# A cross-attention kernel: its four chunks of queries in the order 1, 3, 2, 0 instead of 1, 2, 3, 0

## What is computed

```
q = LN(x) @ Wq.T ; k = ctx @ Wk.T ; v = ctx @ Wv.T            # 16 heads of 16
scores = q k.T / 4 ; masked keys and keys after the query's own row -> -inf
attn = softmax(scores) ; context = attn @ v
x = x + (sigmoid(LN(x) @ Wg.T + bg) * context) @ Wo.T
scale = the two largest of softmax(LN(x) @ gate_w), others 0  # 8 experts
x = x + sum_e (silu(s_e xn @ w1_e) * (s_e xn @ w3_e)) @ w2_e  # xn = LN(x), s_e = its scale
```

## Time and profile before

| | us |
|---|---|
| three runs | 688.59, 688.75, 693.32 (median 688.75) |
| the profiled execution | 690.36 |
| its span, from first to last instruction | 688.6 |
| mean granted TensorE clock, share of full speed | 0.963 |

### The profile page before, as it was taken

How to read it: one execution, slowest core, us unless ns; L and a number is a source line. 1 busy time by engine, 2 the same in 40 slices (tenths; PEclk the granted TensorE clock), 3 DMA queues, 4 the chain that set the end, 5 groups by cost and what they waited for, 6 DMA issues and landing times.

```text
span 688.6 us, 13557 instructions
## 1 busy us (share of the span) xinstructions
PE 653.8 (95%) x5320; PEld 377.0 (55%) x5320; DVE 469.9 (68%) x969; ACT 385.0 (56%) x778; POOL 242.9 (35%) x293
## 2 busy tenths in 40 slices
PE   7897999999989999999999999999999996899996
PEld 3354455455545445444554445545456675688884
DVE  5684778999866999989987975454423354645452
ACT  2212676766634777777566877677875640232331
POOL 5004123422140305020211614527164535566563
PEclk9898999999996999999999999999999998899997
DMA  6984766010700000000770101003010011012000
GB/s 169 242 118 84 130 129 79 2 21 33 114 11 1 3 3 2 2 33 32 96 181 1 35 1 31 2 3 108 2 44 21 16 33 62 31 62 90 34 31 30
DMA packets 29305, 36.58 MB, mean 53 GB/s; under 512 B 5833, under 2 KB 16457, under 8 KB 29242
## 3 DMA queue, kind: packets, MB, share of 16 engines
q1 hardware_dynamic: 26248, 34.53, 23.7%
q10 hardware_dynamic: 946, 0.92, 0.4%
q0 software_dynamic: 2048, 0.27, 0.3%
HBM read 25.58 MB, written 8.06 MB: 49 GB/s over the span
## 4 chain that ended last, share of the span: by engine, by line
PE 74%; POOL 9%; DVE 7%; issue 6%; ACT 4%; POOLq 0%; ACTq 0%; DVEq 0%
PE bank L1566 18%; PE bank L1544 14%; PE bank L1511 11%; PE bank L1395 11%; PE bank L1630 3%; POOL h_lo L1022 3%; POOL v_sb L1018 3%; PE bank L1632 2%; PE bank L1631 2%; DVE pmax L1284 2%; POOL xn_sb L994 2%; ACT probs L1150 2%; PE bank L1515 2%; DVE v_sb L1374 2%; PE bank L1470 2%
## 5 line engine op out<-in xcount | busy, mean ns | idle before, releaser
L1284 DVE TENSOR_REDUCE pmax<-bank 128x1 f32<-128x512 f32 (+6 forms) x640 | 327.5, 578 | 69.3 <-PE bank L1515 46.8
L1150 ACT ACTIVATE probs<-bank 128x512 f32<-128x512 f32 (+4 forms) x592 | 287.4, 545 | 138.0 <-PE bank L1544 86.8
L1566 PE MATMUL bank<-probs,vaug 128*32 128x256 f32 (+4 forms) x2048 | 156.1, 396 | 0.5 <-ACT probs L1150 0.5
L1544 PE MATMUL bank<-qaug,kaug 64*128 64x512 f32 (+4 forms) x592 | 149.0, 452 | 7.0 <-DVE pmax L1284 3.2
L1511 PE MATMUL bank<-kaug,qaug 62*128 62x512 f32 (+6 forms) x640 | 139.6, 414 | 3.1 <-DVE pmax L1284 1.6
L1544 PEld LDWEIGHTS bank<-qaug,kaug 64*128 64x128 f32 (+1 forms) x592 | 64.4, 185 | 82.3 <-ACT probs L1150 29.8
L1511 PEld LDWEIGHTS bank<-kaug,qaug 62*128 62x128 f32 x640 | 70.7, 189 | 56.5 <-DVE pmax L1284 21.3
L1032 POOL TENSOR_SCALAR nmax<-rmax 128x16 f32<-128x16 f32 x16 | 5.2, 323 | 235.3 <-DVE rmax L1292 235.3
L1566 PEld LDWEIGHTS bank<-probs,vaug 128*32 128x32 f32 (+1 forms) x2048 | 46.5, 109 | 52.1 <-issue 31.1
L1202 ACT ACTIVATE h_hi<-v_sb 128x512 fp32r<-128x512 f32 x32 | 20.2, 632 | 80.5 <-DVE v_sb L1374 79.4
L1022 POOL TENSOR_TENSOR h_lo<-v_sb,h_hi 128x512 fp32r<-128x512 f32 x32 | 41.2, 1288 | 61.3 <-ACT h_hi L1202 61.3
(11 more groups left out here) (137 smaller groups left out, 790.2 us busy)
## 6 DMA issues: line engine op xcount, KB each, us to landing
qaug<-s_dram SPq DMA_DIRECT2D x32, 256.0 KB, 3.3
qaug<-q_parts SPq DMA_DIRECT2D x18, 256.0 KB, 9.2
q_parts<-stage SPq DMA_DIRECT2D x7, 512.0 KB, 2.9
k_parts<-stage SPq DMA_DIRECT2D x4, 512.0 KB, 5.3
w_sb<-in_w SPq DMA_DIRECT2D x4, 512.0 KB, 11.0
out<-x_sb SPq DMA_DIRECT2D x8, 256.0 KB, 2.2
ctx_sb<-in_ctx_t SPq DMA_DIRECT2D x3, 512.0 KB, 5.7
x_sb<-in_x SPq DMA_DIRECT2D x3, 512.0 KB, 6.9
```

What stands on the lines that cost most here:

```text
L1150: act.activation(probs[0:rows, u % NSLOT, h, off:CH], bank_of(e)[0:rows, off:CH], ACT.Exp, scale=DK ** -0.5).then_inc(act_read, 1)
L1284: dve.tensor_reduce(pmax[:, n % 2, qt, h, slot:slot + 1], bank[:, 0:w], AX_X, ALU.max).then_inc(dve_read, 1)
L1544: last.append(pe.matmul(pair[side][0][0:r, off:CH], keys_at(b, ROWS, hp, P * j, r), qaug[b:b + ROWS, p % 2, hp, off:CH], start=True, stop= ...
L1566: last = pe.matmul(psum[O_BANK][32 * h:32 * h + 32, q0:q1], vaug[0:r, col:col + 32], probs[0:r, u % NSLOT, h, q0:q1], start=(j == 0), stop ...
```

## The change

The chunks go in the order 1, 3, 2, 0. Position 1 is now chunk 3 and position 2 chunk 2. Chunk 3 needs all keys, so position 1's list holds the projections of key chunks 2 and 3 and value tiles 8 to 12, and position 2's list holds none of these. The two key chunks are read back by one `kload` step: SyncE waits for all four stores, then issues 12 DMAs. The second `kload` step, that of position 2, is gone. All sizes and instruction counts stay the same; `make_plan` is run anew, so the order in which each engine meets its work may differ everywhere.

```diff
-ORDER = (1, 2, 3, 0)
+ORDER = (1, 3, 2, 0)
...
-KEYS_OF = ((0, 1), (2,), (3,), ())
+KEYS_OF = ((0, 1), (2, 3), (), ())
 FIRST_M = (1, 0, 0, 0)
-FIRST_TILE = (0, 8, 12, KT, KT)
+FIRST_TILE = (0, 8, KT, KT, KT)
...
     steps = [*norm]
     for k in KEYS_OF[p]:
-        steps += [("kq", "k", 0, k), ("kq", "k", 1, k), ("kload", p)]
+        steps += [("kq", "k", 0, k), ("kq", "k", 1, k)]
+    if KEYS_OF[p]:
+        steps.append(("kload", p))
```

## The result

The changed kernel takes 702.86 us (median of 4 runs, 700.59 to 708.52); the kernel before, on the same chip, 691.04 (4 runs, 688.59 to 694.45). The ratio is 1.0176, 95% interval 1.0124 to 1.0228: slower by 12 us. The forecast was 690, with a range up to 702.

A forecast was written before the change was run, and what follows sets the result against it. VectorE's maxima were taken to pace the long stretch (126.0 to 420.8 us) and TensorE's experts the end. To the profiled 690.4 us the terms added only 1.7, giving 692.1, or 690 against the median; range 676 to 702.

The forecast's parts named there:

- The loads move into the head: Before group 4: extra key stores and loads delay position 1's queries by at most 8.6 us, covered by 10.1; cost 0.
- Rival 4: In the head: the loads aren't covered and group 4 begins some 4 us late, 694 us; chance 0.05.
- VectorE's term 0: Long stretch, 126.0 to 420.8 us: the same 448 reduces with the same shapes after the swap, so 0 change.
- Exponentials behind larger folds: At group 5: ScalarE waits 0 to 3.4 us for the fold of 64 reduces; 1.7 taken.
- Less left at the end: After the long stretch: 8 fewer exponentials in groups 10 and 11, but 358 still run before 420.8; 0, bound -7.0 us.
- The experts' gate: Group 8's exponentials end 9.9 us later, so the first experts begin near 402 and 434; cost 0, bound 9.9 us.
- Rival 2: From the experts on: their gate decides, experts 0 to 3 come up to 9.9 us late, 700 us; chance 0.20.
- Rival 1: Near 203 us: the new list fills TensorE's wait for position 0's layer norm, gaining 11.9 us, 678.5; chance 0.24.
- Rival 3: One more stall of the kind at 203 us, costing 7.2 us, 697 us; chance 0.07.

The follow-up runs named there:

- fold_first: The changed kernel with SyncE holding position 1's twelve key loads until group 1's fold has landed, all lists kept; 709.70 us, ratio 1.0261.
- split_keys: The changed kernel with key chunks 2 and 3 loaded by separate steps, each after its own stores; 698.77 us, ratio 1.0079.
- k3_late: The changed kernel with key chunk 3's projections, stores and loads behind position 1's queries, the two chunks loaded apart; 695.37 us, ratio 1.0039.
- joint_old_order: The changed kernel with the old order 1, 2, 3, 0 and value tile 12 left in place, both key chunks still loaded together; 706.93 us, ratio 1.0203.
- after_st4: The changed kernel with the scheduler allowed to run four `st` (score tile) items ahead instead of three; 724.94 us, ratio 1.0475.
- big_loads_alone: The changed kernel with key chunk 3's six small loads issued behind the query loads, lists and stores kept; 707.96 us, ratio 1.0231.

## Why the prediction was wrong, point by point

**The step that failed** is "The loads move into the head": the cost put at 0 under a cover of 10.1 us, with a worst case of 8.6. Its first half was right: the key loads went out 8.2 us later (84.22 against 76.03), by two more turns of the stores. But the query loads went out 16.2 us later, not 8.6 at most, and the last of them landed at 131.4. That is 5.4 us after the 126.0 at which group 4 began before, so the cover was gone, and by the step's own rule 5.4 of the 7.2 us would have come from this alone.

Two terms were missing. The step counted SyncE's queue and left the query projections where they were on TensorE. The new list put the first of them 11.1 us later. And the fold of group 1 wasn't in the account, whose four DMAs go out from GpSimd's queue at 88.1 to 89.7, the time to which the large loads had been moved. TensorE waited 4.39 us for it and ran at the lower clock after it. By the same list in fold_first this cost 6.4 us up to group 4's first scores, beside the late queries and not on top of them. Rival 4 named the right place, at 4 us and a chance of 0.05.

What the head costs in all can only be read from kernels whose lists differ: 1.4% (9.5 us) in the new order and 2.0% (14 us) in the old. Group 4's start accounts for 6.3 (133.2 - 126.9) and 7.6 us (136.1 - 128.5) of these. The rest lies behind it, in lists that were made anew, and no run takes it apart. Nor is group 4's start in split_keys (132.1) explained by a wait: its queries are in by 126.2 and the fold holds nobody, but TensorE is busy for 118.9 us up to there, in k3_late for 112.8.

**VectorE's term 0** was right: 449 reduces in 231.96 us, the stretch 0.6 us shorter.

**Exponentials behind larger folds**, 0 to 3.4 us, taken as 1.7: no such wait came. ScalarE's timeline of the kernel after at the change from group 4 to group 5:

```profile
242.63 3.27 ACT L1152 ACTIVATE probs<-bank 65x512 f32<-65x512 f32 x6 [0.41 <-PE bank L1551]
246.47 1.08 ACT L1152 ACTIVATE probs<-bank 128x512 f32<-128x512 f32 x2 [0.56 <-PE bank L1546]
```

The row of six holds the four of group 4's last key tile (65 keys) and two of the next group, without a gap between them, and the next wait is 0.56 us. I had group 4 done at 210.9; the list let it run until 245, and what the next group then waits for is TensorE's scores, no DMA.

**Less left at the end**: the assumption that as many exponentials run beside the maxima (358) was wrong, 331 did. It cost less than the 10.4 us of the second stretch suggest: k3_late left as many (196) and was within 0.4% of the kernel before.

**The experts' gate**: forecast 402 and 434, measured 423.94 and 456.95, of which 7.2 us come from the head. Rival 2 gave 700 by this mechanism. The time comes near, the mechanism doesn't carry it: joint_old_order has the old gate and the whole loss, while k3_late has the new gate, the first expert at 410.25 and the second at 443.74, and nearly none.

**Rival 1**, that the stall after position 0's layer norm goes: it stayed. From 216 to 236 us the clock is 0.57 and VectorE is busy 8.83 of 20 us, after 2.43 us of idle time behind the 4.86 us norm; before it was 12.73 of 20 at 0.68. This stall is longer now, by 3.9 us of VectorE. Rival 3 had one more stall in its place, at 7.2 us.

## What to carry to other kernels

When loads are moved to another time, ask what other transfers are in flight at that time on any queue, and which engine that works in order waits for one of them; the length of the issuing queue alone is not the cost. Follow the whole path of what stands behind the moved work: here the projection on TensorE, the store and its landing, the load and its landing. Where two such waits end at about the same time, as the fold's and the queries' do here, taking away one gives nothing (fold_first). What is needed last goes behind what is needed first: key chunk 3 joined to chunk 2 ahead of the queries cost 1.4 and 2.0% more than loaded apart and behind them. And if two stages share work, compare the sum of both: here a stage longer by 10 us went with a kernel that was 1.8% slower and with one that was 0.4% slower.

## What the runs showed of the hardware

How long group 1's four small DMAs from GpSimd's queue take depends on when the large key loads of SyncE's queue went out. Issued 10 us or more after the last of them, they landed in 2.5 to 2.8 us (k3_late, before); issued 8 us after it, in 4.7 us (split_keys); issued within 2 us of it or while they went out, in 10.2 to 12.5 us (after_st4, big_loads_alone, after, joint_old_order); and with the key loads held back, in 1.6 us (fold_first). SyncE's own small transfers fared alike: key chunk 3's stores took 12 us behind six large loads in split_keys and 2 to 3 us in the kernel after, where they went out ahead of the loads. The key loads themselves landed 4.2 to 13.1 us after issue in both kernels, whether six or twelve went out.

An idle time of TensorE of 2.4 us was followed by 20 us at a mean clock of 0.57 (after) to 0.68, in which VectorE did 11.0 and 7.1 us less than in a quiet stretch. In the kernel after, the clock stays at 1.2 GHz for 16 us behind it, from 220 to 236, though TensorE is busy all that time. These stalls stand in different places in each list. One number of the scheduler alone moved the ratio by -1.3% (k3_late), -0.5% (the change), +0.4% (before) and +0.3% (old order with late keys), so a change that makes the list anew carries as much with it, whatever it is for.
